# Recurrent heads on one core: four heads in one weight load instead of two, with the states in a ring that GpSimd copies out

## What is computed

```
x = tokens * rsqrt(mean(tokens**2) + eps) * norm_w      # (B, T, H, D)
a_t = tanh(a)                                           # (H, S, S)
def step(state, x_t):                                   # state (B, H, S), 512 steps
    state = tanh(einsum('bhs,hst->bht', state, a_t) + einsum('bhd,hds->bhs', x_t, b))
    mixed = einsum('bhs,hsd->bhd', state, c) + skip * x_t
    return state, mixed
return tokens + outs @ w_out.T + b_out
```

## Time and profile before

| | |
|---|---|
| median of 3 runs | 3323.34 us (3321.22 to 3327.7) |
| profiled execution, its own time | 3318.02 us |
| its span | 3316.3 us |
| PE busy | 3032.1 us (91%) |
| DVE busy | 2118.7 us (64%) |
| ACT busy | 1625.0 us (49%) |
| POOL busy | 1100.4 us (33%) |
| states' loop (first to last ACT L1326) | 829.0 to 1412.5 us |

### The profile page before, as it was taken

One profiled execution on the slowest core, in us unless ns is written; L12 is line 12 of the kernel. 1 busy time (PEld: TensorE's weight loads), 2 busy tenths in 40 slices (PEclk: granted clock), 3 DMA queues, 4 the chain that ended last, 5 costly groups with the idle time before them and its releaser, 6 DMA issues. The chain is left out here.

```text
span 3316.3 us, 57926 instructions
## 1 busy us (share of the span) xinstructions
PE 3032.1 (91%) x22345; PEld 1816.2 (55%) x22345; DVE 2118.7 (64%) x4817; ACT 1625.0 (49%) x3321; POOL 1100.4 (33%) x587
## 2 busy tenths in 40 slices
PE   8888899898999999998987888987989889989998
PEld 3333344443999999953434544444454344564547
DVE  6777534545555555556559887778791559945991
ACT  3555432523333333334346777676763557734762
POOL 1111100000000000000028878778770208931990
PEclk8999999999555555589998999999999899999999
DMA  5343332022000000012143322222220201250224
GB/s 153 101 100 95 78 115 79 1 95 72 3 3 3 3 3 3 3 34 72 60 161 97 94 76 88 89 86 87 78 67 0 99 1 53 100 200 4 89 91 189
DMA packets 113490, 234.28 MB, mean 71 GB/s; under 512 B 13760, under 2 KB 50752, under 8 KB 104768
## 3 DMA queue, kind: packets, MB, share of 16 engines
q1 hardware_dynamic: 113216, 230.59, 21.6%
HBM read 185.71 MB, written 44.83 MB: 70 GB/s over the span
## 5 line engine op out<-in xcount | busy, mean ns | idle before, releaser
L2512 DVE TENSOR_TENSOR_SCAN s_hh<-psum,s_dbu 128x512 f32<-128x512 f32 x384 | 447.3, 1207 | 74.3 <-ACT psum L2124 74.1
L2382 POOL TENSOR_TENSOR s_dbu<-s_du,s_bb 128x1024 f32<-128x1024 f32 x191 | 448.0, 2367 | 63.6 <-DVE s_hh L2512 53.1
L1252 PEld LDWEIGHTS psum<-h_now,h_parts 128*128 128x128 f16 x12264 | 446.2, 109 | 6.2 <-DVE h_now L1379 5.4
L1252 PE MATMUL psum<-h_now,h_parts 128*128 128x4 f16 x12264 | 421.2, 168 | 4.5 <-DVE h_now L1379 4.5
L1326 ACT ACTIVATE h_hist<-psum 128x16 f32<-128x16 f32 x1024 | 187.5, 183 | 398.8 <-PE psum L1252 326.2
L1379 DVE TENSOR_SCALAR h_now<-h_hist 128x16 f16<-128x16 f32 x1022 | 188.5, 184 | 216.7 <-ACT h_hist L1326 216.7
L2124 ACT ACTIVATE psum<-s_delta,s_decay 128x512 f32<-128x512 f32 x384 | 256.6, 686 | 107.1 <-DVE s_hh L2512 104.9
L1338 POOL TENSOR_TENSOR h_lay<-w_c,h_xt 128x128 f32<-128x128 f32 x128 | 49.9, 411 | 684.1 <-PE psum L1242 507.4
L2016 PEld LDWEIGHTS psum<-w_c,s_term 128*128 128x128 f32 x1536 | 198.6, 149 | 134.5 <-issue 115.3
L911 DVE TENSOR_TENSOR f_hid<-f_gate,psum 128x512 f32<-128x512 f32 x184 | 126.5, 688 | 206.9 <-PE psum L837 199.6
L898 ACT ACTIVATE f_gate<-psum 128x512 f32<-128x512 f32 x184 | 109.6, 597 | 283.9 <-PE psum L833 283.8
(11 more groups left out here) (527 smaller groups left out, 6169.8 us busy)
## 6 DMA issues: line engine op xcount, KB each, us to landing
s_bb<-s_wide SPq DMA_DIRECT2D x192, 256.0 KB, 3.5
x_spill<-x_flip SPq DMA_DIRECT2D x28, 1024.0 KB, 3.8
f_share<-f_wide SPq DMA_DIRECT2D x208, 128.0 KB, 3.0
s_cc<-s_wide SPq DMA_DIRECT2D x60, 256.0 KB, 3.4
a_ks<-a_spread SPq DMA_DIRECT2D x96, 128.0 KB, 3.3
a_qs<-a_spread SPq DMA_DIRECT2D x96, 128.0 KB, 3.9
x_spare<-x_spill SPq DMA_DIRECT2D x4, 2048.0 KB, 7.6
x_raw<-x_spill SPq DMA_DIRECT2D x4, 2048.0 KB, 7.6
```

Source lines behind the costliest of these rows:

```text
L1252: mm = nc.tensor.matmul(here[:, cols], parts[:, part, GROUP * grp + p, :], now[:, grp, cut, cols], start=False, stop=True, skip_group_chec ...
L2382: nc.gpsimd.tensor_tensor(dbu[:, s % D_RING], du[:, t % 2], both(bb[:, s % B_RING, :]), ALU.mult).then_inc(dbu_ready, 1)
L2512: nc.vector.tensor_tensor_scan(hh[:, s % 4, half, :], DECAYS[i % 3], dbu[:, s % D_RING, half, :], 0.0, ALU.mult, ALU.add).then_inc(scan_do ...
```

## The change

- Four heads make a **quad** and share one 128x128 weight array, one head per quadrant (`a_four`, `parts` now with an index for the parity of the step). A quadrant leads from one half of the partitions to the same or to the other half, so two of the four heads change halves at each step, and there are two arrangements, for even and odd steps (`turned`).
- A quad's state takes 16 columns: four heads by four sequences, each head in its own 4 columns and in one half of the partitions; the other half of those columns is zero. A group is now two quads, 32 columns. `advance` (L1263) runs three products of two matmuls with 16 columns.
- Only the valid half of each column may be written back, so a group's tanh is two ACTIVATEs (L1342) on 64 partitions each, into `ring`, which has 16 steps, is cleared once and keeps its zeros. VectorE (L1427, L1429) reads 32 columns of the ring.
- The history keeps its size. GpSimd copies it out of the ring, four copies per block (`keep`, L1383), each of which waits for the one before; ScalarE waits for the copies of two blocks before (`kept`) when it comes round, and so does TensorE before the first `mix_in` of a piece.
- `put` (L1355) writes 128x256 tiles, `lay_inputs` (L1253) has 128 columns, and `mix_in` (L1280) has 128 columns, 128 matmuls in all instead of 256, with weights `c` for each parity (twice as wide) and pieces of 64 steps. Fillers: one after steps 1 to 4, and one of the mix after steps 5 and 7; none after steps 0 and 6.

```diff
-    PAIRS, S, BLOCK = 8, 64, 8
-    GROUP = PAIRS // 2
-    WIDTH = GROUP * BATCH
-    BLOCKS, SPAN, PIECE = TIME // BLOCK, 128, 32
+    HEADS, QUADS, S, BLOCK = 16, 4, 64, 8
+    GROUP = QUADS // 2
+    PAIRS = 2 * GROUP
+    COLS = GROUP * 4 * BATCH
+    TURN = 2 * BLOCK
+    BLOCKS, SPAN, PIECE = TIME // BLOCK, 128, 64
...
-    MIX_AT = tuple(s for s in range(PIECE) if s % BLOCK not in LAY_AT)
+    MIX_AT = tuple(s for s in range(PIECE) if s % BLOCK in (5, 7))
...
+        ring = sb("h_ring", [P, TURN, 2, COLS])
...
-                        for p in range(GROUP):
-                            cols = slice(BATCH * p, BATCH * p + BATCH)
-                            mm = nc.tensor.matmul(here[:, cols], parts[:, part, GROUP * grp + p, :], now[:, grp, cut, cols],
+                        for q in range(GROUP):
+                            cols = slice(q * 4 * BATCH, (q + 1) * 4 * BATCH)
+                            mm = nc.tensor.matmul(here[:, cols], parts[:, part, i % 2, GROUP * grp + q, :], now[:, grp, cut, cols],
                                                   start=False, stop=True, skip_group_check=True)
...
+                    if s == 0 and blk >= 2:
+                        act.wait_ge(kept, 4 * (blk - 1))
                     for grp in range(2):
                         if i:
                             act.wait_ge(drive[grp], i)
-                        nc.scalar.activation(hist[:, i, grp, :], columns_of(blk, grp)[:, s, :], ACT.Tanh,
-                                             scale=RAISED ** -2).then_inc(state[grp], 1)
+                        for half in range(2):
+                            rows = slice(S * half, S * half + S)
+                            nc.scalar.activation(valid(ring[rows, i % TURN, grp, :], i % 2, half),
+                                                 valid(columns_of(blk, grp)[rows, s, :], i % 2, half), ACT.Tanh,
+                                                 scale=RAISED ** -2).then_inc(state[grp], 1)
...
+                def keep(blk):
...
+                    for grp in range(2):
+                        pool.wait_ge(state[grp], 2 * (blk + 1) * BLOCK)
+                    pool.wait_ge(laid, min(blk + 3, BLOCKS))
+                    start = blk % 2 * BLOCK
+                    for parity in range(2):
+                        for half in range(2):
...
+                            if half:
+                                pool.wait_ge(kept, 4 * blk + 2 * parity + 1)
+                            elif parity:
+                                pool.wait_ge(kept, 4 * blk + 2)
+                            nc.gpsimd.tensor_copy(dst, src).then_inc(kept, 1)
+
+                nc.gpsimd.memset(ring[:], 0.0).then_inc(cleared, 1)
                 pool.wait_ge(x_ready, CHUNKS)
+                for blk in range(2):
+                    put(blk)
                 for blk in range(BLOCKS):
-                    put(blk)
+                    if blk + 2 < BLOCKS:
+                        if blk:
+                            pool.wait_ge(kept, 4 * blk)
+                        put(blk + 2)
+                    keep(blk)
```

More of the change, by code:

```diff
@@ L1208, in recurrent_heads @@
         xt = sb("h_xt", [P, TIME, BATCH])
-        lay = sb("h_lay", [P, 2, 2, BLOCK, WIDTH])
-        now = sb("h_now", [P, 2, 2, WIDTH], F16)
-        hist = sb("h_hist", [P, TIME, 2, WIDTH])
+        lay = sb("h_lay", [P, 2, 2, BLOCK, COLS])
+        ring = sb("h_ring", [P, TURN, 2, COLS])
+        now = sb("h_now", [P, 2, 2, COLS], F16)
+        hist = sb("h_hist", [P, TIME, 2, PAIRS * BATCH])
         mix = sb("h_mix", [P, BATCH, TIME])
@@ L1216, in columns_of, with valid @@
         def columns_of(blk, grp):
-            return bank[2 * (blk % 2) + grp][:, 0:BLOCK * WIDTH].rearrange("p (s c) -> p s c", c=WIDTH)
+            return bank[2 * (blk % 2) + grp][:, 0:BLOCK * COLS].rearrange("p (s c) -> p s c", c=COLS)
+        def valid(x, parity, half):
+            if parity == 0:
+                return x.rearrange("p (k u b) -> p k u b", u=2, b=BATCH)[:, :, half, :]
+            return x.rearrange("p (q v c) -> p q v c", q=GROUP, v=2)[:, :, half, :]
+        own = g.same8.rearrange("p (h e) -> p h e", e=8)[:, :, 0]
         with nc.Block() as block:
@@ L1262, in mix_in @@
                 def mix_in(piece, n):
-                    p, half = divmod(n, 2)
-                    grp, col = p // GROUP, p % GROUP * BATCH
-                    at, per = piece * PIECE + half * HALF, SPAN // PIECE
-                    from_column = (piece % per * PIECE + half * HALF) * BATCH
-                    mm = nc.tensor.matmul(bank[4 + piece // per][:, from_column:from_column + HALF * BATCH],
-                                          w["c"][:, p * P:(p + 1) * P], hist[:, at:at + HALF, grp, col:col + BATCH],
-                                          start=(n == 0), stop=(p == PAIRS - 1), skip_group_check=True)
-                    if n == 2 * PAIRS - 1:
+                    if n == 0:
+                        pe.wait_ge(kept, 4 * (piece + 1) * PIECE // BLOCK)
+                    parity, p = n // (2 * PAIRS), n % (2 * PAIRS)
+                    at, per = piece * PIECE, SPAN // PIECE
+                    home = bank[4 + piece // per].rearrange("p (t b) -> p t b", b=BATCH)
+                    mm = nc.tensor.matmul(home[:, piece % per * PIECE + parity:(piece % per + 1) * PIECE:2, :],
+                                          w["c"][:, (parity * 2 * PAIRS + p) * P:(parity * 2 * PAIRS + p + 1) * P],
+                                          hist[:, at + parity:at + PIECE:2, p // PAIRS, p % PAIRS * BATCH:(p % PAIRS + 1) * BATCH],
+                                          start=(p == 0), stop=(p == 2 * PAIRS - 1))
+                    if n == 4 * PAIRS - 1:
                         mm.then_inc(mix_ready, 1)
@@ L1288, in _ @@
                 warm(nc, g, bank[0], 4)
-                for grp in range(2):
-                    pe.wait_ge(state[grp], TIME)
-                for n in range(2 * PAIRS):
+                for n in range(4 * PAIRS):
                     mix_in(TIME // PIECE - 1, n)
@@ L1362, in _ @@
                 nc.vector.tensor_scalar(w["b"], w["b"], RAISED * RAISED, None, ALU.mult).then_inc(b_raised, 1)
-                a_part = [parts[:, q, :, :].rearrange("p a t -> p (a t)") for q in range(2)]
+                a_part = [parts[:, k].rearrange("p v q t -> p (v q t)") for k in range(2)]
                 dve.wait_ge(weights_bounded, 1)
@@ L3511, in weight_parts, with turned @@
     n = "L1_attn_a_"
-    c_own = np.concatenate([blocks((P, P), [(64 * s, 8 * (2 * p + s), a[n + "c"][2 * p + s]) for s in range(2)])
-                            for p in range(8)], axis=1)
-    a_two = np.concatenate([blocks((P, P), [(64 * s, 64 * s, a[n + "a"][2 * p + s]) for s in range(2)]) for p in range(8)], axis=1)
-    b_two = blocks((P, P), [(8 * h, 64 * (h % 2), a[n + "b"][h]) for h in range(16)])
-    parts["l1a"] = [("a", a_two), ("b", b_two),
+    quads = [[4 * q + k for k in range(4)] for q in range(4)]
+    def turned(q, parity):
+        h0, h1, h2, h3 = quads[q]
+        return (h0, h1, h2, h3) if parity == 0 else (h0, h2, h1, h3)
+    c_own = np.concatenate([blocks((P, P), [(0, 8 * low, a[n + "c"][low]), (64, 8 * high, a[n + "c"][high])])
+                            for parity in range(2) for q in range(4)
+                            for low, high in ((lambda t: ((t[0], t[1]), (t[2], t[3])))(turned(q, parity)))], axis=1)
+    a_four = np.concatenate([blocks((P, P), [(64 * (k // 2), 64 * (k % 2), a[n + "a"][h]) for k, h in enumerate(turned(q, parity))])
+                             for parity in range(2) for q in range(4)], axis=1)
+    b_two = blocks((P, P), [(8 * h, 64 * half, a[n + "b"][h]) for h in range(16) for half in range(2)])
+    parts["l1a"] = [("a", a_four), ("b", b_two),
                     ("c", c_own), ("norm_w", columns(a[n + "norm_w"])), ("skip", a[n + "skip"].reshape(P, 1)),
```

31 lines of the change are left out of this document (20 added, 11 removed).

## The result

The changed kernel takes 3362.51 us, median of four runs (3357.82 to 3366.58); the kernel before took 3322.28 beside it (3320.37 to 3327.7). The ratio is 1.012, 95% interval 1.0103 to 1.0137: **slower by 1.2%**. The profiled execution is the longest of the four, 3366.58, 48.6 us over that of before (3318.0). The comparison of the two traces is made on this pair; the medians lie 40.2 us apart, 8 less than the pair. Executions of one kernel differ by about as much.

The account below looks back on a forecast made before the run. PE's own work was taken to bound filled steps, one group's chain (ACT, DVE, PE) unfilled ones and, after the change, the loop. Terms -57 + 45 + 19 + 0.5 = +7 us on 3323.3 gave 3330 us, range 3268 to 3365.

Parts of the forecast that it names:

- chain, loop without GpSimd: States' loop without GpSimd's work: 511 steps of 1.03 us, 526 against 583, so -57 us.
- second ACT: Chain of one group: issuing ACT twice adds 0.08 us per step, upper bound 0.18.
- the fillers: PE's filler matmuls, 64 to 128 columns: columns cost nothing, 0.50 us each kept, about 0.70 if counted in full.
- put: GpSimd's masked inputs beside VectorE: 0.72 us each (bounds 0.16 and 1.34), 62 in the loop, 45 us.
- keep, and the wait on it: GpSimd's four history copies per block: 0.30 us (bounds 0 and 1.16), 63 times, 19 us; ScalarE's wait at nothing.
- The case stood among the rivals at 0.07: ACT in two halves costs 0.18, not 0.08, per step: +51 us, 3381; chance 0.07.
- Its own sign of it: Loop: unfilled, undisturbed steps over 1.1 us would show that the chain was underrated.
- the cover of 0.08: Filled step: PE is done at 0.95 of the chain's 1.03 us, so the filler hides with 0.08 to spare.
- The small terms: First put +0.5 us; ScalarE's wait on copies, last copies, last mix matmuls and larger weights all at nothing.
- no contention: Loop: GpSimd's work doesn't reach the chain, 526 us of loop, 3267 in all; chance 0.12.
- Half contention: Only VectorE's first operation regularly meets GpSimd: put 0.4, keep 0.15, 34 us in all, 3300; chance 0.18.

Follow-up runs that it names:

- e5: Changed kernel with GpSimd's copies and puts taken out of the loop, ScalarE's halves kept (history zero, later inputs stale): 3330.26 us.
- e6: Changed kernel without GpSimd's copies and puts in the loop, and with both ScalarE instructions of a group on all 128 partitions: 3274.74 us.
- e4: Changed kernel without the four copies per block to the history and without ScalarE's waits on them; puts kept: 3344.58 us.
- e1: Changed kernel with both ACTIVATEs of a group on all 128 partitions instead of 64 each (wrong states): 3312.28 us.
- e3: Changed kernel with group 1's ACTIVATEs in the order upper half, lower half; nothing left out: 3357.74 us.
- e7: Kernel before, with only its fillers changed: half as many, of 128 columns instead of 64: 3295.32 us, ratio 0.993 to the kernel before.
- e2: Changed kernel with one 128x32 ACTIVATE per group for both halves (wrong states); ScalarE's wait became a separate instruction: 3319.57 us.
- e9: Changed kernel with ScalarE's halves on all partitions, masked by a tensor scale, and puts made by ScalarE: 3364.52 us, ratio 1.0127 to the kernel before.

## Why the prediction was right and wrong

The forecast leaned to slower by 7 us, with 0.42 for slower and 0.40 for faster: that the direction came out is luck. The time is inside the range of 3268 to 3365 by 2.5 us only, 3362.5, 32 above the 3330, and it is that near because two errors went against each other: contention was priced 23 us too high, the chain 64 too low. On the profiled executions the change is +48.6 against the sum's +7. The terms, each against its runs (the three lines "of it" are what the chain cost beyond the forecast's 1.03 per step):

```
term                          forecast    measured    from
chain, loop without GpSimd      -57          +7       590.3 (e5) - 583.2 (before)
  of it second ACT past 0.08      0         +53       590.3 - 536.9 (e5, e6)
  of it the fillers               0         +18       (1.051 - 1.016) x 511 (e6)
  of it the rest of the chain     0          -7       (1.016 - 1.03) x 511 (e6)
put                              45          22       (9.60 - 9.25) x 63 (e4, e5)
keep, and the wait on it         19          19       (9.90 - 9.60) x 63 (changed, e4)
sum                              +7         +48
```

- **What binds.** Right: PE's work fell below the chain, PE idles before its bursts, and its clock stayed at 0.50. The chain's other parts held: first to second VectorE operation 1101.99 - 1101.77 = 0.22 (0.21 forecast), and the unfilled undisturbed step of e6 is 1.016 (1.03).
- **The second ACT** is the step that failed, the term "+0.08" of the chain's sum. "Two that waited for nothing last 0.26 together, one 0.18: +0.08 (upper bound 0.18, one after the other)" took the price from two instructions on the same 128 partitions for two on different halves. It is 0.20, a little over the upper bound, and e1, e3, e5 and e6 show that the partitions make the difference. The case stood among the rivals at 0.07, with +51: its size was right (51 to 53), and its chance was far too low. None of its rows shows two neighbours on different partitions, so the two ends deserved equal chances. Its own sign of it came: undisturbed steps without a filler over 1.1 us (1.14, place 6).
- **The fillers.** "The columns cost nothing; I keep 0.50 per filler" was wrong: +0.10 (e7). On the chain every second step is 1.089 for 1.016, where the cover of 0.08 should have hidden the filler; that is 18 us of e6's loop, whose mean step is 1.051. The cover was added up wrongly besides: behind group 0's four first matmuls, at 0.95, its last two have to follow, 2 x 0.027, so PE is done at 1.00 of 1.03 and the cover is 0.03. A filler dearer by 0.10 is over that by 0.07, which is what the long steps show. Under the halves' longer chain it is less, 1.135 and 1.18. The sentence took its price from a row of eight equal matmuls, and no row had one alone between bursts.
- **The puts.** "The stretch is 0.56 longer, and I let all of that show: 0.72" was too much: 0.35. Of four VectorE operations in the stretch one is held, by 0.37 (e4). In the changed kernel the put meets two, one of each group (0.59 and 0.56); with the full rows the two kinds of work cost 9.11 - 8.43 = 0.68 per block together, with the halves 9.90 - 9.25 = 0.65, where the forecast had 0.72 + 0.30 = 1.02.
- **The copies.** 0.30 forecast and 0.30 measured, but not for the copies alone. The operations beside them last 0.28 and 0.32 for 0.18 and 0.19, and the step before them grows too (place 7: 1.245 for 1.18). The timeline credits ScalarE's wait there to the copies (1106.06), but those that ScalarE asks for were done a block before; what shows is the second wait itself, as in e2. The trace has one place with copies and without this wait, the start of block 1, since the wait begins with block 2. That place, and the same one a block later:

```profile
838.43 0.87 PE L1263 MATMUL psum<-h_now,h_parts 128*128 128x16 f16 x12 [0.28 <-DVE h_now L1427]
...
838.68 1.34 POOL L1383 COPY h_hist<-h_ring 64x128 f32<-64x128 f32 x4 [8.20 <-ACT h_ring L1342]
...
838.91 0.80 ACT L1342 ACTIVATE h_ring<-psum 64x16 f32<-64x16 f32 x4 [0.35 <-PE psum L1263]
839.33 0.18 DVE L1427 TENSOR_SCALAR h_now<-h_ring 128x32 f16<-128x32 f32 x1 [0.31 <-ACT h_ring L1342]
```

```profile
848.13 0.86 PE L1263 MATMUL psum<-h_now,h_parts 128*128 128x16 f16 x12 [0.28 <-DVE h_now L1427]
...
848.38 1.34 POOL L1383 COPY h_hist<-h_ring 64x128 f32<-64x128 f32 x4 [7.01 <-ACT h_ring L1342]
...
848.67 0.79 ACT L1342 ACTIVATE h_ring<-psum 64x16 f32<-64x16 f32 x4 [0.41 <-POOL h_hist L1383]
849.09 0.32 DVE L1427 TENSOR_SCALAR h_now<-h_ring 128x32 f16<-128x32 f32 x1 [0.38 <-ACT h_ring L1342]
```

  With the wait ScalarE starts 0.54 after the burst, without it 0.48, as in other steps: 0.06 per block that no copy causes. And the 0.06 moves VectorE's operations against the copies: the steps 7, 0 and 1 take 1.14, 1.14 and 1.68 without the wait, 1.20, 1.41 and 1.52 with it, 0.17 more in all. In e9 the same two places have 1.20 and 1.20 for the steps 7 and 0 without, and 1.26 and 1.44 with; in e1 the three steps come to the same sum, 3.71. So how much of the 0.30 is the copies' and how much the wait's is open: each trace has one such place, and no run took the wait away throughout and left the copies.
- The chain's errors (64 us) were hidden to a third by the contention's, 64 forecast and 41 measured: 64 - 23 = 41 is what the sum was off. **The small terms** held: the loop accounts for 48 of the 48.5 us of span.

Of the rivals, *no contention* would have been right about the time only in a kernel without the halves' cost: e6 gives 3274.7 where it said 3267. *Half contention* came nearest on its own matter: 34 forecast, 41 measured.

## What to carry to other kernels

A price read from two neighbours holds for neighbours of that shape: before it is used on a chain, look whether start partition, operand kinds or position among other work differ, and if no row shows the new combination, give both bounds the same weight. Halving the work of the engine that binds is worth only the distance to the next bound; here the chain stood 0.18 us below PE, and a cheap edit that only thins the fillers (e7) took 23 us of it, while the rebuilt product spent it on a second ScalarE instruction and on GpSimd. Work on GpSimd beside a dependency chain through VectorE cost about a quarter of its own time here (0.35 of 1.27 for a put, and 0.30 of 1.34 for the copies, a wait of ScalarE's included), but what it costs hangs on where VectorE's operations fall: 0.06 us of shift decided whether the copies met them. And an edit for an experiment must leave the form of the instructions beside it alone: e2 priced a separate wait along with the wide instruction.

## What the runs showed of the hardware

- ScalarE instructions of 64 partitions that alternate between the lower and the upper half start 0.203 us apart at 0.179 long, so they don't overlap; with one start partition, 0.08 apart at 0.181. That it is the change of partitions and not their number, e3 shows: there two neighbours on the same 64 partitions start 0.085 apart.
- A ScalarE instruction with a wait in a separate instruction before it starts 0.27 us after the start of the matmul that releases it, and 0.21 after it with its only wait in itself (e1, a block's first state against the others; e2, all states). In e1 and in the changed kernel those 0.06 are paid for a second wait on something long done.
- A scale read from a tensor makes the same instruction 271 ns instead of 181, and two start 0.172 apart.
- A VectorE operation caught by GpSimd ends within 0.04 to 0.05 us after the GpSimd instruction that it met (1108.40 against 1108.36). The Trainium skill ("SBUF — State Buffer", section "Who interferes with whom") calls it an exclusive lock on the ports that the two engines share, held for the whole instruction; the trace agrees for both of VectorE's operations, with up to 0.4 us of waiting.
- A float32 matmul of 128 columns between bursts of short ones keeps PE 0.10 us longer than one of 64, though in a row of equal ones both take 0.21.
